# First input unit in three parts, one half of the convolution matrices loaded, aggregations in banks of their own, second unit turned in two

## The reference, cut to what matters

```
out = conv(x, weight, 9 taps, 4 groups) + (c @ c_weight.T)[:, :, None] + bias[None, :, None]
x = x + out
h = gelu(embedding @ W0 + b0);  h = gelu(h @ W1 + b1)
att = softmax(h @ W2 + b2)
agg_w = einsum('bk,koi->boi', att, weight);  agg_b = att @ bias_k
x = x + einsum('boi,bih->boh', agg_w, x) + agg_b[:, :, None]
```

## Time and profile before

| | |
|---|---|
| Median of 3 runs | 249.48 us (249.44 to 249.81) |
| Profiled execution, its own time | 250.47 us |
| Its span in the trace | 248.7 us |
| PE busy | 238.5 us (96%) |
| DVE busy | 219.7 us (88%) |
| ACT busy | 126.7 us (51%) |
| POOL busy | 10.4 us (4%) |
| Chain that ended last | PE 85%, DMA 6%, DVE 5%, issue 1%, ACTq 1% |

### The profile page before, as it was taken

One profiled execution on the slowest core, in us unless ns is written; L12 is line 12 of the kernel. 1 busy time (PEld: TensorE's weight loads), 2 busy tenths in 40 slices (PEclk: granted clock), 3 DMA queues, 4 the chain that ended last, 5 costly groups with the idle time before them and its releaser, 6 DMA issues.

```text
span 248.7 us, 5771 instructions
## 1 busy us (share of the span) xinstructions
PE 238.5 (96%) x2162; PEld 102.9 (41%) x2162; DVE 219.7 (88%) x112; ACT 126.7 (51%) x208; POOL 10.4 (4%) x36
## 2 busy tenths in 40 slices
PE   7899799999999999999999999999999999999991
PEld 5643234444444444444444444444444444444540
DVE  0165799999999999999999999999999999999582
ACT  2554108354545637374545446373644446273772
POOL 1322300000000000000000000000000000000000
PEclk9799999999999999999999999999999999999997
DMA  7999944999999999998999999999989897444448
GB/s 184 239 303 272 276 94 131 281 275 396 337 342 259 370 253 390 230 373 255 333 302 288 341 238 387 246 397 222 379 254 341 283 289 288 169 169 173 169 181 328
DMA packets 29771, 68.60 MB, mean 276 GB/s; under 512 B 3312, under 2 KB 5744, under 8 KB 29760
## 3 DMA queue, kind: packets, MB, share of 16 engines
q1 hardware_dynamic: 19824, 51.12, 62.2%
q10 hardware_dynamic: 9936, 17.34, 26.4%
HBM read 34.89 MB, written 33.55 MB: 275 GB/s over the span
## 4 chain that ended last, share of the span: by engine, by line
PE 85%; DMA 6%; DVE 5%; issue 1%; ACTq 1%; ACT 0%; DVEq 0%
PE yps L540 60%; PE zps L563 21%; DMA xin<-in_x 4%; DVE xph L412 2%; DMA mlps<-in_mlp 2%; DVE ynat L447 2%; PE yps L577 1%; DVE ycol L438 1%; PE yps L620 1%; PE zps L589 1%; PE yps L600 0%; ACTq L337 0%; PE zps L649 0%; DVE xin L508 0%; PE zps L600 0%
## 5 line engine op out<-in xcount | busy, mean ns | idle before, releaser
L540 PE MATMUL yps<-xph,wraw 64*64 64x512 f32 x1512 | 169.4, 589 | 1.5 <-DVE ycol L438 1.3
L309 ACT ACTIVATE zout<-zps,gamu 128x512 f32<-128x512 f32 x120 | 72.7, 689 | 95.2 <-PE zps L563 79.4
L540 PEld LDWEIGHTS yps<-xph,wraw 64*64 64x64 f32 x1512 | 67.7, 132 | 96.2 <-issue 96.2
L438 DVE STREAM_TRANSPOSE ycol<-yps 128x1024 f32<-128x1024 f32 x63 | 75.0, 1224 | 9.6 <-PE yps L540 8.0
L412 DVE STREAM_TRANSPOSE xph<-xin 128x4160 f32<-128x4160 f32 (+2 forms) x17 | 71.8, 4223 | 3.8 <-DMA xin<-in_x 3.8
L447 DVE STREAM_TRANSPOSE ynat<-ycol 128x4096 f32<-128x4096 f32 x15 | 66.7, 4446 | 1.1
L563 PE MATMUL zps<-ynat,mixv 64*64 64x512 f32 x480 | 57.8, 589 | 0.2 <-DVE ynat L447 0.2
L318 ACT ACTIVATE mixv<-mixt 64x256 f32 (+1 forms) x64 | 42.5, 664 | 1.2
L563 PEld LDWEIGHTS zps<-ynat,mixv 64*64 64x64 f32 x480 | 21.6, 133 | 29.9 <-issue 29.6
L248 POOL COPY gamu<-gam 128x4 f32 (+1 forms) x16 | 2.9, 188 | 196.7 <-ACT zout L309 191.8
L620 PE MATMUL yps<-zout 128*128 128x256 f32 x26 | 9.8, 536 | 1.3 <-POOL zout L250 1.3
(11 more groups left out here) (52 smaller groups left out, 29.7 us busy)
## 6 DMA issues: line engine op xcount, KB each, us to landing
out<-zout SPq DMA_DIRECT2D x60, 512.0 KB, 5.6
xin<-in_x SPq DMA_DIRECT2D x60, 258.0 KB, 7.2
xin<-in_x ACTq DMA_DIRECT2D x60, 258.0 KB, 7.5
out<-xin SPq DMA_DIRECT2D x2, 512.0 KB, 2.7
out<-xin SPq DMA_DIRECT2D x4, 256.0 KB, 3.0
xin<-in_x ACTq DMA_DIRECT2D x4, 132.0 KB, 5.8
xin<-in_x SPq DMA_DIRECT2D x4, 130.0 KB, 6.7
xin<-in_x SPq DMA_DIRECT2D x4, 128.0 KB, 7.6
```

The source lines that it names most:

```text
L309: nc.scalar.activation(zout[:, o].rearrange("p (i c j q) -> p c i j q", i=2, c=2, q=PH)[:, c], zps[:, at:at + BANK].rearrange("p (q i j) - ...
L438: nc.vector.transpose(ycol[:, :, :, :, :, g].rearrange("p i s j q c -> p (i s j) q c"), yps[:, 2 * BANK * (g % 2):2 * BANK * (g % 2) + 2 * ...
L540: last = nc.tensor.matmul(yps[C * c:C * c + C, at:at + BANK].rearrange("p (s f) -> p s f", s=S // 2), wsum[rows, b, g], xph[slot][rows, g, ...
```

## The change

1. Unit 0's input comes in three parts instead of two, cut at phase columns 60 and 95 of 130 (`CUTS`), with a semaphore for each. DVE turns them in three instructions.
2. `wraw` is loaded for 64 partitions; DVE copies it to the other 64. POOL's sum on `wraw` waits for the copy (`w_both`).
3. `mixw` is loaded by ACT instead of SP. ACT's pieces of unit 0 and unit 1 are issued at other places among its activations, and a small exponential on zeros (`spare`) stands ahead of the one of the softmax.
4. The first aggregation goes to `yps` and the second to `zps`, without a wait between them. The first is made and moved out with its rows 2 and 3 ahead of rows 0 and 1. The convolutions, which write the same banks of `yps`, wait for `agg_out`.
5. DVE turns unit 1 in two instructions, with `y_columns(0, 1)` between them. All waits on `turned` count accordingly.

```
+CUTS = 0, 60, 95, 2 * NJ + 2
...
         def x_piece(slot, u, i, k, t, part=None):
 
-            at, to = ((x_from[i], x_to[i]) if part is None else
-                      ((x_from[i], x_cut[i]), (x_cut[i], x_to[i]))[part])
+            at, to = x_from[i], x_to[i]
+            if part is not None:
+                at = max(at, H * i + PH * CUTS[part] - PAD)
+                to = min(to, H * i + PH * CUTS[part + 1] - PAD)
...
-            sp.dma_start(mixw, mix_w).then_inc(mix_in, 16)
-            for part, there in ((0, x_first), (1, x_in[0])):
+            for part in range(3):
                 for k in range(KQ):
                     for t in range(2):
-                        sp.dma_start(*x_piece(0, 0, 0, k, t, part)).then_inc(there, 16)
+                        sp.dma_start(*x_piece(0, 0, 0, k, t, part)).then_inc(x_part[part], 16)
...
-            pool.wait_ge(w_in, 16)
+            pool.wait_ge(w_both, 1)
...
-            def gather(a, i):
-                act.wait_ge(agg_mm, 8 * a + 4 * i + 4)
+            def gather(a, i, n):
+
+                act.wait_ge(agg_mm, n)
...
-            act.dma_start(wraw[:], conv_w).then_inc(w_in, 16)
+            act.dma_start(wraw[0:C], conv_w).then_inc(w_in, 16)
+            act.dma_start(mixw, mix_w).then_inc(mix_in, 16)
+            first_load(0, 0)
+            first_load(0, 1)
             act.wait_ge(zeroed, 1)
             nc.scalar.activation(warm[:], warm[:], ACT.Gelu)
-            for t in range(2):
-                act.dma_start(*x_piece(0, 0, 1, 0, t, 1)).then_inc(x_in[0], 16)
+            first_load(1, 0)
...
             nc.scalar.activation(h2, sps[:, NS:2 * NS], ACT.Gelu, bias=b1s).then_inc(act_mlp, 1)
+            nc.scalar.activation(spare[:], still[:, 0:1], ACT.Exp)
+            first_load(2, 0)
...
-            load_block(1, 1, 0)
+            first_load(2, 1)
...
+            load_block(1, 1, 0)
+            gather(0, 1, 4)
             load_block(1, 1, 1)
-            gather(0, 0)
-            gather(0, 1)
-            gather(1, 0)
-            gather(1, 1)
+            gather(0, 0, 8)
+            gather(1, 0, 12)
+            gather(1, 1, 16)
...
+            dve.wait_ge(w_in, 16)
+            nc.vector.tensor_copy(wraw[C:P], wraw[0:C]).then_inc(w_both, 1)
...
-            first_phases(0)
-            first_phases(1)
+            for part in range(3):
+                first_phases(part)
             y_columns(0, 0)
-            phases(1, 1)
+            second_phases(0)
             y_columns(0, 1)
+            second_phases(1)
...
-                for r in range(RT):
-                    if a > 0 and r % 2 == 0:
-                        pe.wait_ge(agg_out, 2 * a - 1 + r // 2)
+                for r in ((2, 3, 0, 1), range(RT))[a]:
                     for d in range(2):
-                        nc.tensor.matmul(zps[C * d:C * d + C, BANK * r:BANK * r + BANK],
+                        nc.tensor.matmul((yps, zps)[a][C * d:C * d + C, BANK * r:BANK * r + BANK],
...
             keep_on(3)
-            first_aggregate()
+            aggregates()
+
+            pe.wait_ge(agg_out, 1)
             keep_on(3)
-            second_aggregate()
-            pe.wait_ge(w_in, 16)
             pe.wait_ge(w_sum, 1)
+
+            pe.wait_ge(agg_out, 2)
             conv(0, 0, 0)
```

More of the change, by code:

```diff
@@ L76, in build @@
         ones = sb("ones", [1, P])
-        warm = sb("warm", [P, 1])
+        warm, spare = sb("warm", [P, 1]), sb("spare", [P, 1])
         negmax, esum, erec = sb("negmax", [P, 1]), sb("esum", [P, 1]), sb("erec", [P, 1])
@@ L100, in build @@
         x_in = [sem(f"x_in{i}") for i in range(2)]
-        x_first = sem("x_first")
+        x_part = [sem("x_first"), sem("x_second"), x_in[0]]
         z_out = [sem(f"z_out{o}") for o in range(PR)]
@@ L118, in build @@
             sem(n) for n in ("last_conv", "last_cols", "last_nat", "last_mixes"))
-        w_sum = sem("w_sum")
+        w_both, w_sum = sem("w_both"), sem("w_sum")
         mm = sem("mm")
@@ L193, in load @@
                 if not (isinstance(u, int) and u < 2):
-                    sp.wait_ge(turned, u)
+                    sp.wait_ge(turned, 3 if isinstance(u, int) and u == 2 else u + 2)
                 for k in range(KQ):
@@ L294, in load @@
             def load(u, slot):
-                act.wait_ge(turned, u)
+                act.wait_ge(turned, 3 if isinstance(u, int) and u == 2 else u + 2)
                 for k in range(KQ):
@@ L318, in matrices, with first_load @@
                         nc.scalar.activation(mix_places(slot, h, d), mix_values(u, d), ACT.Copy).then_inc(mixv_made, 1)
-            def gather(a, i):
-                act.wait_ge(agg_mm, 8 * a + 4 * i + 4)
+            def gather(a, i, n):
+                act.wait_ge(agg_mm, n)
                 nc.scalar.activation(mixt[:, a, 2 * RO * i:2 * RO * i + 2 * RO].rearrange("p c b -> p (c b)"),
-                                     zps[:, 2 * BANK * i:2 * BANK * i + 2 * BANK], ACT.Copy).then_inc(agg_out, 1)
-            act.dma_start(wraw[:], conv_w).then_inc(w_in, 16)
-            for k in range(KQ):
+                                     (yps, zps)[a][:, 2 * BANK * i:2 * BANK * i + 2 * BANK], ACT.Copy).then_inc(agg_out, 1)
+            def first_load(part, k):
                 for t in range(2):
-                    act.dma_start(*x_piece(0, 0, 1, k, t, 0)).then_inc(x_first, 16)
+                    act.dma_start(*x_piece(0, 0, 1, k, t, part)).then_inc(x_part[part], 16)
+            act.dma_start(wraw[0:C], conv_w).then_inc(w_in, 16)
+            act.dma_start(mixw, mix_w).then_inc(mix_in, 16)
+            first_load(0, 0)
+            first_load(0, 1)
             act.wait_ge(zeroed, 1)
             nc.scalar.activation(warm[:], warm[:], ACT.Gelu)
-            for t in range(2):
-                act.dma_start(*x_piece(0, 0, 1, 0, t, 1)).then_inc(x_in[0], 16)
+            first_load(1, 0)
             act.wait_ge(mlp_in, 16)
@@ L335, in _ @@
             nc.scalar.activation(h1, sps[:, 0:NS], ACT.Gelu, bias=b0s).then_inc(act_mlp, 1)
-            for t in range(2):
-                act.dma_start(*x_piece(0, 0, 1, 1, t, 1)).then_inc(x_in[0], 16)
+            first_load(1, 1)
             act.wait_ge(mm, 2)
             nc.scalar.activation(h2, sps[:, NS:2 * NS], ACT.Gelu, bias=b1s).then_inc(act_mlp, 1)
+            nc.scalar.activation(spare[:], still[:, 0:1], ACT.Exp)
+            first_load(2, 0)
             act.wait_ge(soft, 1)
@@ L385, in _ @@
             act.wait_ge(gam_cut, NU)
-            act.wait_ge(turned, NU)
+            act.wait_ge(turned, NU + 2)
             def evacuate_first(o, c):
@@ L414, in turn_in, with first_phases, second_phases @@
                     xin[slot][:, :, PH * at:PH * to].rearrange("q c (j p) -> q j c p", p=PH)).then_inc(turned, 1)
-            def first_phases(c):
-                if c == 0:
[L419 to L424, removed]
+            def first_phases(part):
+                if part == 0:
+                    dve.wait_ge(margins, 4)
+                dve.wait_ge(x_part[part], 128)
+                turn_in(0, CUTS[part], CUTS[part + 1])
+            def second_phases(c):
+                if c == 0:
+                    dve.wait_ge(x_in[1], 128)
+                turn_in(1, (NJ + 2) * c, NJ + 2 + NJ * c)
             def phases(u, slot):
                 dve.wait_ge(x_in[slot], 64 * u + 128 - 64 * slot)
-                if not (isinstance(u, int) and u < 2):
-                    dve.wait_ge(conv_done, 4 * u - 4)
+                dve.wait_ge(conv_done, 4 * u - 4)
                 turn_in(slot, 0, 2 * NJ + 2)
@@ L529, in conv @@
                 if g == 0:
-                    pe.wait_ge(turned, u + 2)
+                    pe.wait_ge(turned, 3 if isinstance(u, int) and u == 0 else u + 4)
                 if not (isinstance(u, int) and u < 1 and g < 2):
@@ L621, in keep_on, with aggregates @@
                                      start=True, stop=True)
-            def first_aggregate():
+            def aggregates():
                 pe.wait_ge(soft, 7)
                 pe.wait_ge(beta_made, 2)
-                pe.wait_ge(mix_eye, 2)
+                pe.wait_ge(mix_eye, 4)
                 aggregate(0)
-            def second_aggregate():
-                pe.wait_ge(mix_eye, 4)
                 aggregate(1)
@@ L639, in pair_constants @@
             def pair_constants():
+                pe.wait_ge(agg_out, CH)
                 pe.wait_ge(const_out, 1)
@@ L770 @@
     arrays = {
[L771 removed]
+        "x": a["x"], "conv_w": np.concatenate([conv_places(a["L0_cond_weight"]), residual], 1)[:C], "mlp": mlp,
         "share": share, "const_w": const_w, "mix_w": mix_w,
```

2 lines of the change are left out of this document (removed).

## The result

The changed kernel is slower: 251.75 us (median of 6, 251.23 to 254.6) against 249.66, a ratio of 1.0097 with a 95% interval of 1.0066 to 1.0129. Its profiled execution took 251.70 us with a span of 249.9, 1.2 us more than the span before. The ratio stands for 2.4 us. The two profiles show half of that, mostly because the profiled execution of before was itself about 1 us above its median.

What follows compares the result with a forecast made beforehand. PE bounds the body, DVE nearly does, and the change only moves its beginning: 1.6 us from the split turn plus 0.4 from unit 1's earlier arrival make 2.0, so 249.48 becomes 247.5 us, range 246.9 to 250.1.

Steps and rivals of the forecast that it cites:

- the one on ACT's last transfers: Start: ACT's last two transfers of unit 1, issued from 14.75 instead of 11.69 us, were costed at nothing.
- the cover: ACT's queue: two earlier transfers still held, some 3 us at half of 337 GB/s, hide the late issue; otherwise up to 3.1 us.
- The arrival: Start: unit 1's input is there for DVE's turn at 22.3 us instead of 22.70, 0.4 us earlier.
- The small packets: Unit 0's load in three parts: 1,024 more packets, mostly near 550 bytes, costed at 0.3 us.
- both rivals built on them: Unit 0's load: packets cost 2.3 us (249.5 us, chance 0.20), or 4.3 us (251.5 us, chance 0.12).
- slower by the transfers: Unit 0's load: a packet costs the same at any of these sizes, unit 1 arrives at 26.3, time 251.5; chance 0.12.
- The loop: Start: DVE's long turn of unit 1 delays PE, which delays DVE; splitting it gives 1.6 us, 14.53 becoming 12.95.
- mark: The first mix, taken as the body's beginning: at 37.23 us before, forecast at 35.25, 2.0 us earlier.
- the later route: From first convolution or arrival to first mix, the later counts: PE's list done at 35.0 us, DVE's at 35.1.
- PE's wait ahead of group 3's convolution: Start: PE's 1.33 us wait for banks that the second ycol frees was forecast to be gone.
- The first convolution: Start, behind PE's zeros: at 17.3 us instead of 17.97, 0.7 earlier; alone gives nothing but is needed.
- Hidden as forecast: Start: DVE's copy (at most 1.25 us, in idle time) and the small exponential (at most 0.2 us) cost the chain nothing.

Runs made afterwards that it cites:

- e1_act_early: The changed kernel with ACT's four transfers of unit 1 issued ahead of the products with the softmax weights; 249.14 us, ratio 0.997 to before.
- e5_before_act_late: The kernel before with only ACT's four transfers of unit 1 issued as late as in the changed kernel; 255.51 us, ratio 1.0224.
- e8_half_early: The changed kernel with only the first two of ACT's four transfers of unit 1 issued earlier; 250.36 us, ratio 1.0051 to before.
- e4_split_only: The kernel before with only unit 1 turned in two instructions, the second ycol between them; 248.53 us, ratio 0.9953.
- e10_zeros: e7_split_early with three more matmuls on zeros in PE's two gaps during the softmax network; 248.40 us, ratio 0.995 to before.
- e11_split_late: The kernel before with the split turn of unit 1 and ACT's late issues of unit 1 as in the changed kernel; 252.43 us, ratio 1.0083.
- e7_split_early: e4_split_only with ACT's last two transfers of unit 1 issued earlier, beside its first two; 248.14 us, ratio 0.9953 to before.
- e12_other_rows: e7_split_early with ACT's four transfers of unit 1 in the other order of channel blocks; 248.44 us, ratio 0.9938 to before.
- e3_one_queue: The changed kernel with SP issuing all eight transfers of unit 1 and ACT none; 253.06 us in 4 runs, no ratio given.
- e2_sp_late: The changed kernel with SP waiting for the softmax weights before it issues its half of unit 1; 253.09 us, ratio 1.0129 to before.

## Why the prediction was wrong

**The step that failed** is the one on ACT's last transfers: "The queue then still holds the two before them [...], so I cost this at nothing". The queue held them, but they were not served. SP's four of unit 1 had been issued ahead of them (from 10.22 us), and ACT's came behind. I had priced the cover by half of 337 GB/s, as if both queues drained side by side. They drained one after the other, each at 198 GB/s. My own reading of the profile could have warned me: the chain of before stands on the transfer that ACT issues at 12.30, the last of the four, and this is the very issue that the change moves.

The arrival came 3.20 us late against before and 3.6 us against forecast. My bound without the cover was 3.1 us, but that it lies near is luck. It counted how much later the last two are issued, 14.75 instead of 11.69. In fact they went out from 15.91, and the first two, which the prediction left out, were moved as well, from 9.1 to 12.4 us, behind the products with the softmax weights. e1_act_early shows this cause undone and e5_before_act_late shows it alone. e8_half_early agrees, but doesn't show it by itself.

**The small packets** were costed rightly, against both rivals built on them. From 9 to 12 us the changed kernel passed 1503 - 166 = 1,337 data packets in 3 us, 446 a us, where 1 KB packets had passed at 239, at 248 GB/s against 258. Unit 0's last part came 0.25 us earlier; the forecast was 0.4. So the rival that landed nearest in time (slower by the transfers, 251.5) had the wrong mechanism. The Trainium skill's rule of 512 B for line rate ("DMA: Bandwidth & Descriptors", section "Specifications") fits these rows so far: packets of some 550 bytes moved about as fast as those of 1 KB. Its 138 GB/s for a transfer of 64 KB (same page, section "Bandwidth") is not what the parts of 70 KB showed with many in flight, 248 GB/s.

**The loop** of DVE and PE was right: forecast 12.95 us from arrival to mark, 12.58 measured, and e4_split_only gave 1.2 us alone where 1.1 was expected. The 0.37 us between them is in DVE's own instructions, which I had costed a little too long back to back: the second half of the turn holds the chain for 2.19 us instead of 2.31, and the three `ycol` for 3.40 instead of 3.59. PE was never the later route with unit 1 so late. PE's wait ahead of group 3's convolution, forecast gone, is 1.89 us, because the `ycol` that it waits for stands behind the late half turn.

**The first convolution** came at 18.48, not 17.3:

```profile
8.84 2.93 PE L632 MATMUL yps<-zout 128*128 128x256 f32 x6
...
11.99 2.75 PE L632 MATMUL yps<-zout 128*128 128x256 f32 x6
14.67 1.11 PE L533 MATMUL yps<-zout 32*64 32x512 f32 x16
```

The zeros stand ahead of work on the chain, and at half clock (granted 0.50 from 8 to 14 us) three of them take 2.93 and 2.75 us instead of 1.56. I took the start of the aggregations (13.52) as given; it was 14.67. By itself this cost nothing here, since unit 1 was later still. But it is how the softmax, the zeros and the clock came to set the issue of unit 1, on the chain above. What made the clock fall sooner in this execution stays open; e10_zeros did not settle it.

**Hidden as forecast:** DVE's copy of `wraw` took 0.59 us in an idle stretch, the small exponential moved nothing (the real one stood at 9.15), and the body is unchanged.

Taken together, in the two profiles: 3.20 us lost by the late arrival, 1.95 gained by the split turn, and nothing that can be told from the rest (e11_split_late at 1.0083 beside 1.0097, with 1 us of room). The split turn alone, or with ACT's issues together (e4_split_only, e7_split_early, e12_other_rows, 0.994 to 0.995), beats both kernels. Still open are why one queue alone is slower, and how much of the loss hangs on the softmax being late in an execution.

## What to carry to other kernels

When a transfer's issue is moved, ask what the other queue has issued ahead of it, not only what its own queue still holds; the transfers of one buffer want to be issued side by side on both queues. An issue behind a compute instruction makes the arrival hang on that instruction's chain, and on everything that may slow it. Where two engines hold each other up by one long instruction, cutting it in two and putting the other's need between is worth testing alone first.

## What the runs showed of the hardware that I had not expected

- **One queue alone gets 198 to 224 GB/s with all engines busy; two can get 337 to 350.** Seen with SP alone, ACT alone, and one queue over all partitions. No run got the higher rate from one queue, but two are not always enough: both had work at 234 GB/s in the kernel before, from 21 to 25 us, and at 231 in e1_act_early, from 15 to 18. Why is open. The Trainium skill, "DMA: Bandwidth & Descriptors", section "Issuing engines are not separate DMA queues", says that issuing from several engines only saves issue time; these runs differ.
- **Two queues are served about in the order of issue.** In the changed kernel nothing of ACT's was moved from 15 to 18 us, behind SP's earlier issues, and in e2_sp_late the other way round. It is no strict order: in the kernel before ACT's last two, issued at 11.69 and 12.30, shared the engines from 16 us on with SP's last ones, issued by 9.98. The same page, section "Queues, rings and completion order", has each engine take turns between the queues that have work; by that rule ACT's transfers of 12.40 would have run beside SP's. The trace differs, with none of ACT's packets from 15 to 18 us.
- **PE's clock after a wait.** Ahead of group 3's convolution PE stood 1.89 us in the changed kernel, and the convolution took 2.81 us at a granted clock of 1.00. After 2.45 us (e3_one_queue) and 3.40 us (e2_sp_late) it took 4.50 us both times, at 0.62 on average, and after 4.53 us (e5_before_act_late) 5.40 us at 0.50. A late buffer can thus cost more than its lateness: in e2_sp_late unit 1 came 0.11 us earlier than in the changed kernel, and the mark 1.40 us later.
